# Experts of one group laid between the attention steps of the next, in one unrolled program

## What is computed

```python
# layer 0
q, k, v = split_heads(xn @ Wq.T + bq), ... (ctx)          # 16 heads of 16
attn = softmax(where(mask == 0, NEG, q k^T / 4)); y = (attn v) @ Wo.T + bo
w = routing_weights(xn1, Wr, temperature)                  # dense: a weight for each of 8 experts
out = sum over e of w[e] * ((silu(xn1 @ Wg[e]) * (xn1 @ Wu[e])) @ Wd[e])      # 256 -> 256 -> 256
# layer 1
single-head attention (256 wide) with a float mask; then a top-1 switch of 8 experts, 256 -> 1024 -> 256, capacity 256
```

## Time and profile before

| | |
|---|---|
| median of 3 runs | 819.97 us (817.18 to 822.01) |
| span of the profiled execution | 819.8 us; its own time isn't given apart, and the median lies within 0.2 us of it |
| instructions | 13407 |
| busy: VectorE, ScalarE, POOL | 504.7, 262.0, 221.3 us |
| DMA | 43.88 MB, mean 54 GB/s |

### The profile page before, as it was taken

The page is one execution under the profiler, slowest core; times in us unless marked ns, Lnnn a source line. Parts: engine busy times, 40 slices in busy tenths (PEclk is TensorE's granted clock), DMA queues, the critical chain, the costliest instruction groups (busy, mean ns, idle before and its releaser), DMA issues.

```text
span 819.8 us, 13407 instructions
## 1 busy us (share of the span) xinstructions
PE 687.0 (84%) x4468; PEld 554.2 (68%) x4468; DVE 504.7 (62%) x1260; ACT 262.0 (32%) x439; POOL 221.3 (27%) x130
## 2 busy tenths in 40 slices
PE   4688869878889888999999999999786672399995
PEld 3344635645555567888888888889575561399995
DVE  4786676677484555655555555756578876266662
ACT  3223323232232332322323322332332332156551
POOL 0254145334226200112022020600102213256451
PEclk9759878977887897999999999999988785599998
DMA  7340000000000200011010200000112141766510
GB/s 216 106 131 2 1 26 0 0 0 0 0 0 1 78 1 1 1 40 38 0 38 0 102 0 0 1 1 2 52 52 86 37 148 39 243 203 227 179 65 25
DMA packets 28130, 43.88 MB, mean 54 GB/s; under 512 B 2543, under 2 KB 21359, under 8 KB 28096
## 3 DMA queue, kind: packets, MB, share of 16 engines
q1 hardware_dynamic: 26032, 37.29, 13.7%
q0 software_dynamic: 2064, 6.16, 2.2%
HBM read 35.19 MB, written 8.45 MB: 53 GB/s over the span
## 4 chain that ended last, share of the span: by engine, by line
PE 68%; DVE 18%; issue 6%; ACT 2%; DMA 2%; SPq 1%; DVEq 1%; POOL 1%; ACTq 0%; POOLq 0%
PE psum L1309 43%; PE psum L1701 6%; PE psum L1405 3%; DVE scratch L277 2%; PE psum L1413 2%; DVE scratch L278 2%; DVE work L279 2%; PE psum L1431 2%; PE psum L1399 2%; PE psum L1609 1%; PE psum L1580 1%; PE psum L1378 1%; PE psum L1443 1%; DMA scal<-in_temp 1%; PE psum L1640 1%
## 5 line engine op out<-in xcount | busy, mean ns | idle before, releaser
L1309 PE MATMUL psum<-arena 128*128 128x256 f32 (+1 forms) x2448 | 428.3, 336 | 26.7 <-DVE arena L755 8.7
L1309 PEld LDWEIGHTS psum<-arena 128*128 128x128 f32 x2448 | 372.8, 196 | 73.6 <-issue 17.2
L1737 POOL TENSOR_TENSOR diag<-neg_ident,work 128x1024 fp32r<-128x1024 f32 x32 | 60.7, 1897 | 118.0 <-DVE work L871 117.9
L801 DVE TENSOR_TENSOR arena<-work,arena 128x512 fp32r<-128x512 f32 x64 | 48.5, 757 | 46.6 <-ACT arena L515 46.6
L515 ACT ACTIVATE arena<-work 128x512 fp32r<-128x512 f32 x64 | 40.4, 632 | 107.4 <-DVE work L799 107.4
L799 DVE TENSOR_TENSOR work<-work,psum 128x512 f32<-128x512 f32 x64 | 43.8, 685 | 43.7 <-ACT work L510 27.8
L551 ACT ACTIVATE work<-psum 128x1024 f32<-128x1024 f32 x32 | 32.8, 1024 | 111.6 <-PE psum L1413 111.6
L1792 POOL CAST arena<-work 128x1536 fp32r<-128x1536 f32 x6 | 8.8, 1473 | 211.0 <-PE psum L1309 211.0
L1066 DVE SCALAR_TENSOR_TENSOR x_all<-psum,w_cur,x_all 128x256 f32<-128x256 f32 x128 | 53.0, 477 | 19.3 <-PE psum L1309 18.3
L510 ACT ACTIVATE work<-psum 128x512 f32<-128x512 f32 x64 | 37.9, 592 | 71.9 <-PE psum L1309 71.8
L1701 PE MATMUL psum<-arena 128*128 128x256 f32 x384 | 47.9, 284 | 0.0
(11 more groups left out here) (187 smaller groups left out, 801.5 us busy)
## 6 DMA issues: line engine op xcount, KB each, us to landing
work<-in_w SPq DMA_DIRECT2D x16, 1024.0 KB
work<-in_w SPq DMA_DIRECT2D x8, 768.0 KB, 4.4
work<-in_ctxT SPq DMA_DIRECT2D x8, 512.0 KB, 4.8
slots<-fill POOLq DMA_DIRECT2D x1, 2080.0 KB
out<-x_all SPq DMA_DIRECT2D x4, 512.0 KB, 3.4
x_all<-slots SPq DMA_DIRECT2D x1, 1560.0 KB, 12.3
x_all<-in_x SPq DMA_DIRECT2D x1, 1536.0 KB, 15.0
work<-in_wa SPq DMA_DIRECT2D x4, 256.0 KB, 6.9
```

Source lines behind the costliest of these rows:

```text
L801: dve.tensor_tensor(hT[i // 2 % 2][1][:, i % 2, :], gu_h[i % 2], hT[i // 2 % 2][0][:, i % 2, :], ALU.subtract).then_inc(hl.sem, 1)
L1309: mm = pe.matmul(dst, left(i, k), right(j, k), start=(n == 0), stop=(n == 3 * K2 - 1))
L1737: pool.tensor_tensor(diag[u % 2], neg_ident[:, :].rearrange("p (o q) -> p o q", o=1).to_broadcast([P, 8, P]), mx[u % 2].rearrange("p (h o) ...
```

## The change

The layer 0 attention and its experts become one program, unrolled over STEPS = 21 steps. Step b holds: the scores of sequence b (b < 16), the values and the whole tail of sequence b-1, and two expert passes, numbers 2(b-4)-1 and 2(b-4) of 32 (pass n is group n // 8, expert n % 8). So the experts of group 0 begin in step 4, when its four sequences are through, and steps 17 to 20 hold experts only.

- K, V and Q are projected for two sequences at a time (half h, `HT` = 256 tokens), one projection each in odd (K) and even (Q, V) steps, with two buffers for K, Q, V and the inputs. Their norm (`norm0`) is for two sequences too.
- The 8 PSUM banks are named: MX (2 banks, scores for the maximum; also logits), ST (2 banks, shifted scores), TL (1 bank, shared by values, tail and the projections), GA, UP and DN (1 each: gate, up, down). There were two pairs of banks for shifted scores, and two banks each for gate and up. There is one diagonal buffer instead of two.
- An expert's weights are loaded and split again for each group, 32 times; POOL splits gate and up, and down, in separate instructions between the diagonals.
- Routing is done per group (32 columns instead of 128), at the end of steps 4, 8, 12 and 16; ScalarE's exponentials for it too.
- The norm after the attention takes 8 chained instructions for its root instead of 11.
- `x_norm3(0)` and the first context of layer 1 come in step 19.
- All loops of this part are unrolled, on all engines; semaphores count from 0 up.

Parts of the diff (hide_for_max(u + 1) waits for maximum(u), hide_shifted(u) for exponential(u - 1), shift(u) for diagonals(u)):

```diff
             def scores(u):
+                if u + 1 < UNITS:
+                    hide_for_max(u + 1)
+                hide_shifted(u)
+                if u + 1 < UNITS:
+                    scores_for_max(u + 1)
+                scores_shifted(u)
+                shift(u)
...
-            def gate_up(g, i):
-                e, n, m = i // 8, i // 2 % 4, i % 2
+            def gate_up(n, m):
+                g, i = n // E, 2 * n + m
+                if m == 0:
+                    pe.wait_ge(gu_lo, n + 1)
+                    if n % E == 0:
+                        pe.wait_ge(x1_lo, GB * g + GB)
+                if i:
+                    pe.wait_ge(sl, i)
...
+            def gate_up_split(n):
+                i = n % 2
+                pool.wait_ge(s_raw2[i], 16 * (n // 2) + 16)
+                if n >= 2:
+                    pool.wait_ge(up, 2 * (n - 2) + 2)
+                pool.tensor_copy(w2s[i][0][:, 0:GU], raw[i][:, 0:GU]).then_inc(gu_hi, 1)
+                pool.wait_ge(gu_hi, n + 1)
+                pool.tensor_tensor(w2s[i][1][:, 0:GU], raw[i][:, 0:GU], w2s[i][0][:, 0:GU], ALU.subtract).then_inc(gu_lo, 1)
```

More of the change, by code:

```diff
@@ L986, in _, with normalise @@
-            for c in range(2):
-                v_add(0, c)
-            for m in range(2):
-                q_low(0, m)
-            for u in range(2):
-                maximum(0, u)
-            small_ready()
-            with dve.Fori(0, G - 1) as g:
-                units(g, g + 1)
-            units(G - 1, None)
+            def normalise(b, n, dst, done):
+                dve.tensor_scalar(dst, x_all[:, b, 0:D], mv[:, n, 0:1], rstd[:, n:n + 1], ALU.subtract, ALU.mult
+                                  ).then_inc(done, 1)
@@ L1556, in pair2 @@
-            def pair2(g, last):
-                for c in range(NC2):
-                    down(g, c)
-                    if c < NC2 - 2 or not last:
-                        gate_up(g, 2 * c + 4)
-                        gate_up(g, 2 * c + 5)
-            pe.wait_ge(s_inh, 1)
-            with pe.Fori(0, E // 2 - 1) as g:
-                pair2(g, False)
-            pair2(E // 2 - 1, True)
+            v_project(0, UP)
+            pe.wait_ge(s_wa_lo, 3)
+            q_project(0, DN)
+            pe.wait_ge(k_lo, 2)
```

1424 lines of the change are left out of this document (695 added, 729 removed).

## The result

The changed kernel takes 891.12 us in the median of four runs (887.04 to 894.34), the kernel before 820.99 beside it: 1.085 times as long, 95% interval 1.079 to 1.091. Forecast were 852, with a range of 812 to 890. The sign and the mechanism were right, the size was not: +70 instead of +32.

A forecast was written before the change was run, and what follows sets the result against it. Experts were taken as bound by TensorE, attention by a ring of short steps among four engines. Steps, routing and end summed to 607.5 us against 573.8, +33, less 1 for an early norm: forecast 852, range 812 to 890.

The forecast's parts named there:

- (a): End of a step, steps 5 to 12: values waits behind VectorE's accumulates, h_low and v_add or xn_low, 2.4 us.
- (b): Odd steps: the next pair's norm0 stands ahead of x1_low in VectorE's queue, so k_project stalls 4.2 us.
- (c): POOL's port holds VectorE's small steps: 2 us more in odd steps at norm0, 1 us elsewhere.
- (d): Odd steps: TensorE's granted clock falls to 0.50 after a 6 us stall, 3 us lost.
- (e): Steps 0 to 4, attention almost alone: a long chain at clock 0.75, 17.5 to 28 us a step, ending at 151.
- The table loads: ScalarE, full steps: four loads of 1.28 us as exp and silu alternate, 5.1 us, within ScalarE's 15.4 against TensorE's 28.5.
- (g): Steps 16 to 20: 23 us for step 16, 16.8 each for 17 to 19 with TensorE alone, 12.5 for step 20.
- (f): Routing four times instead of once: 8 us at a step's end, stalling TensorE 3 us each, 12 in all.
- A: Rival: TensorE stays the only bound, full step near 29.5, total 755, or 785 to 805 with half; chance 0.17.
- B: Rival: it evens out at 812 to 830, with 34 us an odd step and a fill at 20; chance 0.13.
- C: Rival: VectorE behind POOL becomes the bound, 39.7 us a step, +79, total 929, half of it 890; chance 0.10.

The follow-up runs named there:

- end_order: Changed kernel with h_low and v_add or xn_low ahead of the last accumulate in VectorE's queue at a step's end: 883.0 us, 1.081.
- norm_early: Changed kernel with the next pair's norm0 at the end of the preceding even step, behind v_add, instead of ahead of x1_low: 864.5 us, 1.051.
- attn_only: Changed kernel without any layer 0 expert (no loads, splits, products or accumulates), leaving only the attention's own order: 684.9 us in a single run.
- fill_banks: Changed kernel with projections of steps 0 to 3 in the experts' unused banks and issued earlier, two norms moved earlier too: 866.6 us, 1.054.
- warm_fill: Changed kernel with 19 extra mask products a step on TensorE in steps 1 to 3, into a bank nobody reads: 881.5 us, 1.071.
- one_table: Changed kernel with exp of a scaled input in place of the experts' silu, so ScalarE keeps one table: 889.0 us, 1.075.
- pool_light: Changed kernel with POOL's splits of experts 2 to 31 cut to 8 columns, loads, waits and order kept: 861.5 us, 1.054.
- no_routing3: Changed kernel without the routing arithmetic of group 3 (its exps and all but one VectorE step): 881.1 us, 1.072.
- norm_late: Changed kernel with the next pair's norm0 moved in VectorE's queue from before x1_low to behind h_mult: 889.5 us, 1.088.
- tail_order: Changed kernel with three edits behind the last score: two POOL splits wait for x1_transpose, last routing cut in two, stage 3's norm in step 20: 883.0 us, 1.075.
- best2: Changed kernel with the norm, step-end, fill and end reorderings combined, then remaining waits mended, such as cutting the second gate_up in halves: 832.3 us, 1.0095.

## Why the prediction was right or wrong

**Right in its mechanism.** The steps of the middle were priced from rows of a kernel in which no such step existed, and came to 285 for 291. Part of that closeness is luck: steps 6, 7, 10 and 11 took 4.4 us less than the sum, the four that hold a routing or stand behind one 10.8 more. (a) 2.4 us at a step's end: 2.26 and 2.22; half of it was not the accumulate, though, but what is left to do for the one bank (end_order). (b) 4.2 us behind the norm: 4.30 without POOL's splits. (c) 2 us of the port: the norm took 6.1 for 4.1 us. Removing (b) and (c) at once (norm_early) took 6 to 8 us from the odd steps 7 and 11. (d) the clock was at 0.50 for 5.4 us behind the wait of an odd step, and 0.91 over the whole of it, where the sum had 3 us. (e) the fill: 25 us a step, ending at 155.3 for 151; it is the order and not the start (attn_only), the shared bank or the place of the projections in the queue (fill_banks), and the clock (warm_fill), which was 0.64 where 0.75 had been chosen. For steps 1 to 4 the sum has 100.7 us, and executions of the same steps took 98.9 to 107.6, so the 4 us are no more than these differ by.

**The table loads** at nothing: right within what a run can tell (one_table).

**The term that failed is (g).** "Step 16: two passes, tail, wait for x1_low(16): 23. Steps 17 to 19: TensorE alone, 16.8 each, 50. Step 20: 12.5", with 3 of (f): 88.5. It measured 115.5. TensorE alone was a count of its work, not a walk through the queues as in (a) to (d), and it left out or priced too low three waits: the residual's chain (5.6; priced at 2 or so inside the 23), which has no scores over it in step 16 and runs beside POOL's split; the last routing, 10.6 us of small steps on VectorE (562.7 to 573.3), for which the sum had put 3 us, with silu of expert 25 behind it on ScalarE; and the early norm (4.3), which I had booked as a gain of 1. TensorE waits 21.7 us in all, about 6 of them forecast, so 16. The other 11 are mostly clock: it is busy 93.9 us, where the sum has 82.5, at 0.84, 0.94 and 0.91, and the forecast took 1.00 for "TensorE alone"; by these clocks the 93.9 are 84.6 us at 1.00, so some 9 are the clock's.

Of single causes two were shown to their size, waits and clock together. One is POOL's splits, which (c) priced for the odd steps and "elsewhere" but (g) not at all: without them the stretch is 12 to 15 us shorter (pool_light). The other is the last routing, 8.4 us (no_routing3). The two overlap, since steps of that routing are themselves held by a split (2.22 us for one of 32 columns, 0.19 for most), and what they are worth together was not measured. The norm is 3.6 there and nothing in the total; the residual's 3.5 are shown as a wait, not in the total.

**(f)** was too small also in the middle, and partly in the wrong place. It put its 3 us behind the routing, in steps 5 and 9, and these took 40.6 and 40.9 us for 38 + 3. But the routed steps 8 and 12 themselves took 37.3 and 37.4 for 31.7. They hold the products of the logits, and a 2.45 us wait of the new group's first gate_up, which by the order of the queues is for x1_low; the sum has neither.

**The rivals.** A assumed that the queues would not bind, and B that the fill would go at 20 us a step; the queues did bind, and a step of the fill took 25 to 32. C gave the total (890 and above) by another cause: VectorE is busy 22.4 us of an odd step's 36.9, and with the splits gone the total falls by 30, not by the 79 that C had to carry. (852 and 79 are 931, not the 929 of its text.) The Trainium skill (SBUF — State Buffer, Who interferes with whom) has the shared pair of ports held for a whole instruction by whoever issues first. The trace agrees on one side: VectorE's steps end with POOL's instruction. Of POOL being held as well it shows little, its subtraction of 1024 columns taking 2470 ns in the mean, 2340 at the shortest and 2730 at the longest.

## What to carry to other kernels

Before interleaving a latency-bound stage with a throughput-bound one, price the ends as carefully as the middle: in the fill and behind the last scores the new order runs without its cover, and each queue must be walked through there too. A chain of tiny VectorE steps costs what POOL does beside it, so place it where POOL rests, not merely where VectorE does. When a wait is removed and the time stays, look at the next handover before giving the theory up: here three edits in turn (norm_late, tail_order, best2) uncovered the next wait, and all edits together were worth 75 us.

## What the runs showed that was not expected

A norm of eleven two-column steps took 4.0, 4.8, 6.1 or 9.3 us, by what POOL did beside it: nothing, a diagonal, a diagonal and one split, or 9.2 us of work without a pause. Adding 57 products to TensorE in steps 1 to 4 made the stretch 5 to 14 us shorter, the granted clock 0.91 instead of 0.64. Removing 48 table loads, 62 us of ScalarE, changed the total by no more than the runs can tell. And in two traces of the same kernel the same 240 products of steps 17 to 19 kept TensorE busy 45.5 and 43.0 us, at a granted clock of 0.94 and 0.99, which bounds what a single trace can say of the end.
